# Two transformer layers on one core: the feed-forward and second-layer work of a batch laid beside the next batch's attention, with row maxima taken over two score tiles at a time

## The reference

```
x = L0_attn_x                                    # (4, 512, 128)
# 1: softmax attention, 16 heads of 8, rope on q and k
attn = softmax(einsum('bhqd,bhkd->bhqk', q, k) / sqrt(8));  y = (attn @ v) @ W_out + b_out
x = layernorm(x + y)
# 2: 16 experts of 64 hidden (grouped top-k gate, 4 used) and a shared expert of 128
g = silu(x @ w1_e.T); u = x @ w3_e.T
y = einsum('tef,ehf,te->th', g * u, w2_e, combine) + shared(x)
x = layernorm(x + y)
# 3: linear attention, features elu(p @ R) + 1 of 32 per head, on q and k
y = (q' @ (k'^T v)) / max(q' . sum(k'), 1e-6) @ Wo + bo
x = layernorm(x + y)
# 4: base product plus 8 low-rank experts of rank 16, softmax gate, top 2
y = x @ W + b + gated low-rank part
x = layernorm(x + y)
```

## Time and profile before

| what | value |
|---|---|
| median of 3 runs | 628.48 us (627.59 to 629.42) |
| span of the profiled execution | 623.1 us |
| TensorE busy | 499.6 us (80%), mean granted clock 0.868 |
| VectorE busy | 404.9 us (65%) |
| ScalarE busy | 214.9 us (34%) |
| GpSimd busy | 109.1 us (18%) |
| DMA | 20.58 MB, mean 33 GB/s |
| first score product, first exponential's scores | 34.66 us, 64.56 us |

### The profile page before, as it was taken

How to read it: one execution, slowest core, us unless ns; L and a number is a source line. 1 busy time by engine, 2 the same in 40 slices (tenths; PEclk the granted TensorE clock), 3 DMA queues, 4 the chain that set the end, 5 groups by cost and what they waited for, 6 DMA issues and landing times. The chain is left out here.

```text
span 623.1 us, 7805 instructions
## 1 busy us (share of the span) xinstructions
PE 499.6 (80%) x2872; PEld 235.1 (38%) x2872; DVE 404.9 (65%) x1015; ACT 214.9 (34%) x276; POOL 109.1 (18%) x101
## 2 busy tenths in 40 slices
PE   5142993299975999379989989999999999988962
PEld 2010230133322334133334355444554565654651
DVE  6663773088852899349797588977556656656454
ACT  0100262065642666236546712232232313223210
POOL 9770000075050510001000000000000100111120
PEclk9565597599996999769999999999899979968775
DMA  2221328101110011100000000000000000000001
GB/s 97 77 105 65 108 72 197 81 10 52 48 81 26 2 52 66 82 10 2 2 2 2 1 1 1 0 2 0 1 1 1 1 0 1 1 18 0 18 1 34
DMA packets 9422, 20.58 MB, mean 33 GB/s; under 512 B 2082, under 2 KB 7336, under 8 KB 8680
## 3 DMA queue, kind: packets, MB, share of 16 engines
q1 hardware_dynamic: 9384, 20.08, 9.5%
HBM read 15.68 MB, written 4.19 MB: 32 GB/s over the span
## 5 line engine op out<-in xcount | busy, mean ns | idle before, releaser
L1010 DVE TENSOR_REDUCE negmax<-psum 128x1 f32<-128x512 f32 x256 | 169.5, 685 | 101.5 <-PE psum L465 100.6
L734 ACT ACTIVATE probs<-psum 128x1024 f32<-128x1024 f32 x128 | 126.8, 1023 | 163.3 <-PE psum L481 161.2
L465 PE MATMUL psum<-KS,QS 96*128 96x512 bf16 x256 | 104.7, 420 | 38.0 <-DMA QS<-parts_dram 29.7
L481 PE MATMUL psum<-QS,KS 99*128 99x512 bf16 x256 | 80.2, 398 | 46.4 <-DMA QS<-maxp 46.2
L500 PE MATMUL psum<-probs,VA 128*32 128x256 f32 x1024 | 84.8, 397 | 0.6 <-ACT probs L734 0.6
L708 PE MATMUL psum<-xT,late 128*128 128x512 f32 x144 | 71.7, 622 | 0.0
L465 PEld LDWEIGHTS psum<-KS,QS 96*128 96x128 bf16 x256 | 25.6, 100 | 121.7 <-DVE negmax L1010 59.6
L389 POOL TENSOR_SCALAR var<-mv 128x4 f32<-128x4 f32 x16 | 3.7, 229 | 286.6 <-DVE mv L906 286.5
L481 PEld LDWEIGHTS psum<-QS,KS 99*128 99x128 bf16 x256 | 24.8, 102 | 69.5 <-DMA QS<-maxp 47.1
L870 DVE TENSOR_TENSOR QS<-QS,psum 128x512 f32<-128x512 f32 x64 | 43.7, 682 | 2.4 <-PE psum L708 0.4
L829 ACT ACTIVATE QS<-psum 128x512 f32<-128x512 f32 x36 | 21.5, 597 | 65.6 <-PE psum L708 65.6
(11 more groups left out here) (150 smaller groups left out, 599.6 us busy)
## 6 DMA issues: line engine op xcount, KB each, us to landing
KS<-parts_dram SPq DMA_DIRECT2D x3, 1152.0 KB
QS<-parts_dram SPq DMA_DIRECT2D x9, 384.0 KB
parts_dram<-parts SPq DMA_DIRECT2D x8, 384.0 KB, 2.9
late<-in_late SPq DMA_DIRECT2D x1, 2956.0 KB, 15.1
out_y<-KS SPq DMA_DIRECT2D x4, 256.0 KB, 2.2
KS<-parts_dram SPq DMA_DIRECT2D x1, 864.0 KB
QS<-parts_dram SPq DMA_DIRECT2D x3, 288.0 KB
QS<-maxp SPq DMA_DIRECT2D x48, 4.0 KB, 1.7
```

The source lines that it names most:

```text
L465: mm(sm_bank(u)[:, :], QS[b % 2][0:KROW, h, qt * P:(qt + 1) * P], KS[b % 2][0:KROW, h, :], start=True, stop=True).then_inc(sm_full, 1)
L481: last_ = mm(ps[2 * hf + j][:, :], KS[b % 2][0:KROW + 3, h, kt * P:(kt + 1) * P], QS[b % 2][0:KROW + 3, h, :], start=True, stop=True)
L734: fn(probs[:, n % 2, 2 * hf:2 * hf + 2, :], psum[:, 2 * hf:2 * hf + 2, :], ACT.Exp, scale=float(DH) ** -0.5).then_inc(exp_done, 1)
L1010: V.tensor_reduce(out=negmax[:, G % 4, i:i + 1], in_=sm_bank(u)[:, :], axis=X, op=ALU.max, negate=True).then_inc(sm_free, 1)
```

## The change

The kernel is rewritten around one list. `walk_of_work` writes an order of work over 256 units, one for each score tile, and every engine walks the same list and takes its own part of each entry. Unit t holds the scores of tile t (`S`), one tile now, not two; at odd units the pair of score tiles for the maxima (`M`), 24 tiles ahead (`LOOK`) instead of 36; every fourth unit the values (`PV`) of four tiles, as four products of 512 columns. `TEMPLATE` says at which unit after the end of a batch's attention each later step of that batch stands: heads at 5 to 8, the feed-forward steps from 20 to 51 (`G`, `U`, `C`, `D`), the second layer from 58 to 110. So feed-forward and most of the second layer of a batch stand beside the attention of the next, and those of the last batch behind all attention.

Row maxima: the two tiles of a pair go to banks 2 and 3, and one reduce reads both (128 x 2 x 512) and writes two maxima. The next pair may be written only after this reduce. Scores go to banks 0 and 1 in turn, each with its own exponential of 512 columns. Values have bank 4, the feed-forward sum bank 5, and everything else shares banks 6 and 7 in turn until the score banks come free at the end. A group's maxima are split by GpSimd before the transposing product (one bf16 product now), ScalarE copies the result, and three DMAs write the rows as before.

There is one `QS` and one `KS`, and the feed-forward tiles have memory of their own. The stacks have 72 rows and no zero rows. They are laid out in DRAM by head group: each group is stored by six DMAs of 96 KB, with every part written three times, and loaded by two of 288 KB, once the group's scores of the batch before are done. The late weights come in five DMAs instead of one.

Second layer: keys and queries are projected first (`kT`, `qT`), then multiplied by the random matrix in two row tiles of 64; the features are max(v, 0) + exp(min(v, 0)), for which ScalarE takes four steps (two Relu, two Exp) a pair of banks, and VectorE two. The bias products are gone. `O` computes outputs and normalisers with tokens on the partitions, and `OT` is gone. The normalisation moves from VectorE to GpSimd. The start has one memset of stack rows instead of six.

The core of the diff:

```diff
-AHEAD = 2 * HG * NT + 4
+UNITS = GROUPS * HG * NT
+LOOK = 24
+KROW = 9 * DH
+SROW = KROW + 3
...
+TEMPLATE = ((5, "heads", 0), (6, "heads", 1), (7, "heads", 2), (8, "heads", 3), (10, "attnT", 0), (12, "proj", 0),
+            (15, "norm0", 0), (18, "resT", 0), (19, "gate", 0), (27, "combine", 0),
+            (52, "chunk", 0), (54, "norm1", 0), (58, "x2T", 0), (59, "kT", 0), (60, "qT", 0), (61, "V", 0),
+            (62, "K", 0), (63, "Kv", 0), (64, "K", 1), (65, "Kv", 1), (66, "Q", 0), (67, "Qv", 0), (67, "KV", 0),
+            (68, "Q", 1), (69, "Qv", 1), (71, "O", 0), (72, "O", 1), (75, "AT", 0), (77, "Y1", 0), (80, "norm2", 0),
+            (83, "x3T", 0), (92, "lg", 0), (104, "ghT", 0), (106, "Y2", 0), (109, "norm3", 0), (110, "save", 0))
...
+    at = defaultdict(list)
+    for b in range(NB):
+        own, base = HG * NT * NG * b, HG * NT * NG * (b + 1)
+        if b == 1:
+            for off, kind, i in ((-22, "rope", 0), (-21, "rope", 1), (-20, "rope", 2), (-19, "rope", 3), (-10, "split", 0),
+                                 (-4, "split", 1), (-3, "store", 0), (3, "store", 1), (8, "val", 0)):
+                at[off].append((kind, b, i))
+        if b >= 2:
+            for off, kind, i in ((11, "rope", 0), (12, "rope", 1), (13, "rope", 2), (14, "rope", 3), (15, "val", 0),
+                                 (16, "split", 0), (19, "split", 1), (20, "store", 0), (24, "store", 1)):
+                at[own - 64 + off].append((kind, b, i))
+        if b:
+            for g in range(NG):
+                at[own - 64 + 27 + 16 * g].append(("stacks", b, g))
+        at[own + 20].append(("bout", b, 0))
+        for off, kind, i in TEMPLATE:
+            at[base + off].append((kind, b, i))
+        for k in range(PAIRS):
+            g = base + (23 + 3 * k if k else 20)
+            at[g].append(("G", b, k))
+            at[g + 1].append(("U", b, k))
+            if k:
+                at[g + 2].append(("D", b, k - 1))
+                at[g + 2].append(("C", b, k))
+        at[base + 51].append(("D", b, EP))
+    for i, t in enumerate((1, 3, 8, 11, 13)):
+        at[t].append(("late", 0, i))
+
+    order = []
+    for t in range(-LOOK, max(at) + 1):
+        if 0 <= t < UNITS:
+            order.append(("S", t, 0))
+        u = t + LOOK
+        if u < UNITS and u % 2 == 1:
+            order.append(("M", u // 2, 0))
+            if u % 16 == 15:
+                order.append(("mx", u // 16, 0))
+        if u % 16 == 2 and 16 <= u < UNITS + 16:
+            order.append(("max", u // 16 - 1, 0))
+        if t % 4 == 2 and 6 <= t <= UNITS + 2:
+            order.append(("PV", t // 4 - 1, 0))
+        if t % 16 == 3 and 16 < t < UNITS + 16:
+            order.append(("OU", t // 16 - 1, 0))
+        order += sorted(at[t], key=lambda s: s[0] not in ("G", "U", "C", "D"))
+        order.append(("step", t, 0))
+    return order
...
+            if kind == "S" and b == 0:
+                spare = [6, 7]
+            if kind == "M" and b == UNITS // 2 - 1:
+                uses[2].append(("M", UNITS // 2 - 1, 0))
+                uses[3].append(("M", UNITS // 2 - 1, 0))
+                spare = [6, 7, 2, 3]
+            if kind == "OU" and b == GROUPS - 1:
+                uses[0].append(("S", UNITS - 2, 0))
+                uses[1].append(("S", UNITS - 1, 0))
+                uses[PVB].append(("OU", GROUPS - 1, 0))
+                spare = [6, 7, 2, 3, 0, 1, 4]
...
+            def store_group(b, i, g):
+
+                src = parts[32 * g:32 * (g + 1), i, :, :]
+                for n in range(3):
+                    if i == 0:
+                        dst = stack_dram[b, 0, g, 24 * n:24 * (n + 1)].rearrange("(p d) j t -> p (d j) t", p=3)
+                    else:
+                        dst = stack_dram[b, 1, g].rearrange("(p n d) j t -> p n (d j) t", p=3, n=3)[:, n]
+                    sp.dma_start(dst.rearrange("p c t -> c p t"), src).then_inc(stack_st[g], 16)
...
+            def load_group(b, g):
+                sp.wait_ge(stack_st[g], 96 * (b + 1))
+                if b:
+                    sp.wait_ge(s_full, 64 * (b - 1) + 16 * (g + 1))
+                else:
+                    sp.wait_ge(init_pool, 2)
...
+                    dst = (KS, QS)[i][0:KROW, HG * g:HG * (g + 1), :].rearrange("r h t -> r (h t)")
+                    sp.dma_start(dst, stack_dram[b, i, g].rearrange("r j t -> r (j t)")).then_inc(qk_ld[g], 16)
...
             def scores_for_max(u):
                 G, i = divmod(u, HG * NT)
-                b, h, qt = G // NG, HG * (G % NG) + i // NT, i % NT
-                if i == 0 and G == 0:
-                    pe.wait_ge(qk_first, 64)
-                if i == 0 and (G == 1 or G and G % NG == 0):
-                    pe.wait_ge(qk_ld[b % 2], 64 * (b // 2 + 1))
-                if G == 0 and u >= 6:
-                    pe.wait_ge(sm_free, u - 5)
-                if G:
-                    pe.wait_ge(sm_free, u - 3 if u < HG * NT + 2 else u - 1)
-                mm(sm_bank(u)[:, :], QS[b % 2][0:KROW, h, qt * P:(qt + 1) * P], KS[b % 2][0:KROW, h, :],
-                   start=True, stop=True).then_inc(sm_full, 1)
-            def scores(w):
-                n, hf = divmod(w, 2)
+                b, g = divmod(G, NG)
+                h, qt = HG * g + i // NT, i % NT
+                if i == 0:
+                    pe.wait_ge(qk_ld[g], 32 * (b + 1))
+                if u >= 2 and u % 2 == 0:
+                    pe.wait_ge(sm_free, u // 2)
+                last_ = mm(ps[2 + u % 2][:, :], QS[0:KROW, h, qt * P:(qt + 1) * P], KS[0:KROW, h, :],
+                           start=True, stop=True)
+                if u % 2:
+                    last_.then_inc(sm_full, 1)
+
+            def scores(t):
+                n, j = divmod(t, HG)
+                G, kt = divmod(n, NT)
+                h = HG * (G % NG) + j
+                if t % 16 == 0:
+                    pe.wait_ge(maxrow_ld[G % 2], 48 * (G // 2 + 1))
+                if t >= 2:
+                    pe.wait_ge(exp_done, t - 1)
+                mm(ps[t % 2][:, :], KS[0:SROW, h, kt * P:(kt + 1) * P], QS[0:SROW, h, :],
+                   start=True, stop=True).then_inc(s_full, 1)
+
+            def values(n):
                 G, kt = divmod(n, NT)
                 b = G // NG
-                if w == 0:
-                    pe.wait_ge(init_dve, 3)
-                    pe.wait_ge(sm_free, HG * NT)
-                if kt == 0 and hf == 0:
-                    pe.wait_ge(maxrow_ld[G % 2], 48 * (G // 2 + 1))
-                if w >= 2:
-                    pe.wait_ge(exp_done, w - 1)
-                for j in range(2):
-                    h = HG * (G % NG) + 2 * hf + j
-                    last_ = mm(ps[2 * hf + j][:, :], KS[b % 2][0:KROW + 3, h, kt * P:(kt + 1) * P],
-                               QS[b % 2][0:KROW + 3, h, :], start=True, stop=True)
-                last_.then_inc(s_full, 1)
-            def values(n, half):
-                G, kt = divmod(n, NT)
-                b = G // NG
-                q = slice(half * T // 2, (half + 1) * T // 2)
-                if half == 0:
-                    pe.wait_ge(exp_done, 2 * n + 2)
-                    if n % (NG * NT) == 0:
-                        pe.wait_ge(v_done, b + 1)
-                        pe.wait_ge(init_pool, 4)
-                    if kt == 0 and G:
-                        pe.wait_ge(o_evac, G)
+                pe.wait_ge(exp_done, HG * (n + 1))
+                if n % (NG * NT) == 0:
+                    pe.wait_ge(v_done, b + 1)
+                    pe.wait_ge(init_pool, 3)
+                if n == 0:
+                    pe.wait_ge(init_dve, 1)
+                if kt == 0 and G:
+                    pe.wait_ge(o_evac, G)
                 for j in range(HG):
                     h = HG * (G % NG) + j
-                    last_ = mm(ps[6][32 * j:32 * j + 32, q], VA[b % 2][:, kt, h, :], probs[:, n % 2, j, q],
-                               start=(kt == 0 and half == 0), stop=(kt == NT - 1), tile_position=(0, 32 * j),
-                               skip_group_check=True)
-                if half:
-                    last_.then_inc(pv_done, 1)
-            def base_layer(b):
+                    last_ = mm(ps[PVB][32 * j:32 * j + HV, :], VA[:, b % 2, kt, h, :], probs[:, n % 2, j, :],
+                               start=(kt == 0), stop=(kt == NT - 1), tile_position=(0, 32 * j), skip_group_check=True)
+                last_.then_inc(pv_done, 1)
...
+            def features(b, i):
+
+                for half, u in enumerate((("Ka", b, i), ("Kb", b, i))):
+                    wait_free(pe, u)
+                rows = (slice(0, 64), slice(64, 128))
+                for t in range(2):
+                    for half, u in enumerate((("Ka", b, i), ("Kb", b, i))):
+                        k = slice((2 * i + t) * P, (2 * i + t + 1) * P)
+                        ins = mm(bank_of(u)[:, t * 256:(t + 1) * 256], kT[rows[half], k], c_["rbd"][rows[half], :],
```

(31 more changed lines are left out.)

1147 lines of the change are left out of this document (464 added, 683 removed).

## The result

The changed kernel takes 720.36 us (median of 4 runs, 716.28 to 729.15); beside it the kernel before took 628.04 (627.43 to 629.42). The ratio is 1.146, with a 95% interval of 1.138 to 1.155. The profiled execution spans 714.8 us. The forecast was 597, with a range up to 638. Executions of one kernel differ by some per cent with the granted clock; the ratios here are of each kernel's faster executions, the medians of all.

| stage | forecast, us | measured, us |
|---|---|---|
| start to first score tile | 60.5 | 54.8 |
| tiles 0 to 63 | 68 | 68.0 |
| tiles 64 to 255 | 335 | 425.9 |
| from the last scores to the end | 128 | 166.1 |
| from the profiled span to the median | 5.4 | 5.6 |

A forecast was written before the change was run, and what follows sets the result against it. Attention was held back by score-stack loads and VectorE's maxima, feed-forward by TensorE alone. Stages 60.5 + 68 + 335 + 128 = 591.5 us of span, plus 5.4 to the median, gave 597 us, range 585 to 622 (0.48), up to 638 in the result.

The forecast's parts named there:

- Prices of the added instructions: Whole kernel: 1.22 us per reduce of 1024, 3.5 us a batch each for K'V and the new output step.
- rival C: Row maxima: the paired reduce costs twice the single one, 19 us at most; 604 to 616 in all; chance 0.10.
- The new wait: Row maxima: a score pair's single buffer makes a chain of 1.92 us a pair, the bound where no side work runs.
- The start: Before the first scores: first load lands near 31, then 12 pairs at half clock; scores start at 60.5 us.
- Tiles 64 to 255: Attention beside feed-forward and second layer: 275 us of TensorE work plus uncovered stalls, 335 us taken.
- (a) Features: Second layer: four feature steps' round trips through TensorE, ScalarE and VectorE stall 8 us a batch, 17 in all.
- (b) GpSimd: Tiles 64 to 255: rotary chains and splitting stand ahead of the normalisation in GpSimd's queue, 14 us in all.
- The end: After the last scores: 38 us to routing weights, 27 for experts, 63 from x2T on; 128 us in all.
- rival D: Clock stays at half through pauses at each pair: tiles 0 to 63 +24, the end +30; 650 us; chance 0.08.
- B: Mixed stretch: feed-forward pairs' tanh waits on VectorE stall TensorE, 2.5 us for 27 pairs; 393 us, 655 in all; chance 0.17.
- A: Mixed stretch: stalls are absorbed, 284 us as in the feed-forward stretch; 546 in all, 545 to 580 with stalls; chance 0.17.
- The gain I counted on: Attention stretch: slow score-stack loads made TensorE wait 46.2 us for rows of maxima; no such wait over 3 us should remain.

The follow-up runs named there:

- the spaced kernel: Changed kernel with normalisation on VectorE, rotary steps of batches 2 and 3 behind it, and second-layer feature steps further apart: 634.0 us, ratio 1.011.
- the run with a quarter of K'V: Changed kernel with one of four row blocks summed in K'V, 12 of 16 products a batch left out: 691.41 us, ratio 1.104.
- both repairs: Changed kernel with normalisation back on VectorE and rotary steps of batches 2 and 3 moved 11 tiles later: 672.57 us, ratio 1.075.
- moving the routing: The spaced kernel with routing 2 to 3 tiles earlier, four steps a tile and not six: 635.24 us, ratio 1.015.
- The repairs: Changed kernel with all three: normalisation on VectorE, later rotary steps, second-layer feature steps further apart: 634.0 us, ratio 1.011.
- the one attempt on it: Three-repair kernel with early routing and one-tile maxima, batch 2's query features and later steps moved behind batch 3's gate: 641.95 us, ratio 1.021.
- the loads alone: Kernel before, score-stack loads split into copies with slowest dimension 24 or 8 rows in place of 3, order unchanged: 592.72 us, ratio 0.947.
- filler run: Changed kernel with useless float32 products, 12 a batch, ahead of TensorE's waits in the second layer's feature steps: 730.54 us, ratio 1.170.
- the one-tile kernel: Three-repair kernel with row maxima again over one tile, 256 reduces of 128x512: 637.99 us, ratio 1.019.

## Why the prediction was wrong, step by step

- **Prices of the added instructions: right.** The reduce of 1024 took 1223 ns (1.22 forecast), so rival C is out. At full clock K'V took 3.66 us (in the spaced kernel) and a half of the new output step 1.87 (the changed kernel's first one), 3.5 and twice 1.75 forecast. VectorE was relieved by 47.6 us and not by some 60; the pairing gave 13 of them (169.5 to 156.5) and not 19.
- **The new wait: right.** Tiles 0 to 63 took 68.0 us, 68 forecast, and at full clock one pair follows another by 1.9 to 2.0 us (77.44, 79.35, 81.31), 1.92 forecast. That the total fits to the microsecond is in part luck, as the 77.4 us in the run with a quarter of K'V show.
- **The start: right in kind.** 54.8 us against 60.5, bounds 57 to 70. The first score product for maxima came at 27.1 us, where I had the load near 31. The rule of the Trainium skill, "DMA: Bandwidth & Descriptors", section "Why a DMA increments its semaphore by 16 and not by 1", would have given 57 and was the nearer one; the kernel before with its slowest dimension at 24 and 8 rows and not 3 agrees with it (share 0.76 for 0.18), as far as the number of loads plays no part.
- **Tiles 64 to 255: the step that failed.** (a) Features: I took "8 us a batch, 17 in all". The idle time was of that size, 13 us. What was missing is that the engine goes on at half clock after it, for most of the next 30 to 40 us, over K'V, the output step, values and scores; this term I had put at nothing. Spacing the steps gave back 30 us here. (b) GpSimd: I took 14 us, and "0.4 us longer twice" for the normalisation. It is 798 ns an instruction on GpSimd against 341 on VectorE (median, in the run that has it there), so 3.1 us against 1.4 for each of 16, and TensorE waited at 10 of them (24.3 us at six places in this stage, 23.4 at the end); with the queue in front, both repairs gave 32 us here (425.9 to 394.1). (c) Of the 91 us over the forecast, these two explain 62. The remaining 29 are mostly in tiles 80 to 95, 144 to 159 and 208 to 223 (36.0, 47.3 and 38.0 us in the spaced kernel, where 16 tiles at 1.75 are 28), beside routing and transposes; moving the routing took 3 of them, and the cause of the rest stays open.
- **The end: failed.** 166 us in place of 128. TensorE was busy for 106.7 us of it, at clock 0.66, where I had 68 us of work (rival D). The last routing weights came 57 us after the last scores in place of 38, the experts took 34 in place of 27, the normalisation behind them 7, and from x2T on it was 69 in place of 63. The repairs took it to 148. The normalisation gave 11 of it, all idle time, and the spacing 7. The other 20 is the chain at clock 0.69, which the one attempt on it did not shorten.
- **The rivals.** D named the half clock, but for tiles 0 to 63 and the end, where I had looked for it in the earlier trace rows; at the end it held, in tiles 0 to 63 not in this profile. The mixed stretch, which has the round trips, I left at full clock. That is where most was lost. B came nearest to the measured time of that stretch (393 against 426) by a mechanism that was wrong: VectorE waited 10.4 us in all for the tanh. A is out.
- **The gain I counted on was real.** In the old order the loads alone give 30 us. The changed kernel lost that and 92 us more, so its order and split of work cost some 122 to 128 us against the kernel with the loads alone.

## What to carry to other kernels

In a fixed order across batches, price a round trip by two things: its idle time, and the half clock that TensorE works at behind it. Where a chain of short steps goes TensorE, ScalarE, VectorE and back, put at least its length in other work between two of its steps; here three tiles in place of two, the read two tiles later and K'V seven tiles behind the keys' features were worth some 38 us with the same instructions. And before an order is rewritten, try the part that the profile names (here loads that ran on few DMA engines) by itself: it alone beat both kernels.

## What the runs showed of the hardware

- Behind one pause of 1.9 us the granted clock fell from 1.00 to 0.50, though TensorE was busy for 13.3 of the 14 us before it (filler run).
- The same work can keep the clock in one execution and lose it in another. In tiles 0 to 63, with pairs and the same order, it stayed at 1.00 from 67 to 130 us in the spaced kernel, and fell to 0.50 from 85 to 112 us in the run with a quarter of K'V; the waits of TensorE just before, 0.68, 0.76 and 0.47 us, are the same in both. With one-tile maxima it fell several times. What tells these apart no run here shows. The Trainium skill, "TensorE: Matmul & The Clock Gate", section "A second HAM failure mode: psum-queue depth-cycling", describes short idling between groups that makes the clock swing; the one-tile kernel and the quarter run agree, the spaced kernel with pairs, which idles as often, does not.
- VectorE's normalisation instruction takes 341 ns (median of 64), but the four at 154.61 us took 2.75 us, 688 each, while GpSimd split rotary results. The Trainium skill, "SBUF — State Buffer", section "Who interferes with whom", says that such an instruction and GpSimd can lock each other out of a shared pair of ports; this row agrees.
- The same form on GpSimd took 798 ns, 2.3 times VectorE's.
